# Small products of the identity on TensorE in the idle places of the opening's plan

## The chip, the cores and the metric

The kernel runs on one NeuronCore of a Trainium2 chip. The metric is the time of one execution on the device in microseconds (us). Engines are named as in the profile: PE is TensorE's matmul, PEld its weight load, DVE is VectorE, ACT is ScalarE, POOL is GpSimd, SP is SyncE.

## The reference

The input x has 8 sequences of 256 tokens with 512 features, 2048 tokens in all. Four blocks are added to it one after the other, each on a layer norm of the current x:

```python
x = x + attn_a(layernorm(x))   # here "the stack": 4 layers, 64 wide
x = x + ffn(layernorm(x))      # weights w * (su @ sv), inner 1792, silu(gate) * up, down
x = x + attn_b(layernorm(x))   # 32 query heads, 8 key/value heads of 128, ALiBi, causal
x = x + ffn(layernorm(x))
```

The stack projects 512 features to 64 and then does four times: layer norm, silu, a causal convolution with a complex decaying exponential along the sequence, layer norm, a small feed-forward of 64 to 256 to 64. At the end it norms and projects back to 512 features. All of it is a long chain of small steps.

## The kernel before

The program has three phases. **Phase 1** does the stack, the first feed-forward and what the attention needs ahead; phase 2 is the attention; phase 3 the second feed-forward. No scheduler of a framework orders them. The kernel has a planner of its own, the class `Steps`: a step has a key (name, a, b), an engine, an assumed duration in us, the steps that it comes after, an urgency and the PSUM places that it takes. `Steps.ordered` goes through the steps by assumed time and gives each engine a fixed order, `order1`. It also keeps `ends`, the time at which each step is assumed to end. Each engine then issues its instructions in that order and waits on semaphores before each step. The plan's times decide the order alone; on the chip a step starts when its semaphores allow.

The 2048 tokens are worked on in four blocks of 512. `stack_steps` makes the steps of one block s of the stack. Block 0 is the lead (`lead`), since the first block of the feed-forward can start only when the lead's last layer is done; the blocks 1 to 3 fill in behind. The steps of PE in a layer are, with their lines: `var` (L1900, two products with 128x128 weights and 2 moving columns, for the variance), `rtr` (L1909, four products that spread the reciprocal root), `conv` (L1919 and L1921), `w1` (L1930), `w2` (L1942), and in the lead `idc` (L1914) and `idw` (L1935), which bring the residual in. Between them stand steps of the other engines: `sq` and `silu` and `hid` on ACT, `eps`, `yn`, `ur`, `zr`, `zi`, `pr` on DVE, `rstd`, `ui`, `pi` on POOL. `xT` (L1885) transposes a block's input, `proj` (L1893) projects it, `out` (L1952) projects back. `fxT` (L1810) transposes the normed result for the feed-forward. `scale` (L1794, L1797) makes the low-rank factors of the feed-forward's weights, and `vecc`, `b1f`, `boutf` (L1867, L1872, L1877) fold biases.

The feed-forward's products (`gate`, `up`, `down`) all go through the helper `mm3` (L828), which takes each product as three passes over a high and a low part:

```python
PASSES = ((0, 0), (0, 1), (1, 0))
...
            for stat, mov in pairs:
                for a, b in PASSES:
                    ins = pe.matmul(out_ap, stat[a], mov[b], start=start and n == 0, stop=stop and n == last)
```

Its first two passes thus have the same stationary operand, one right behind the other.

An f32 matmul of the source that is no transpose stands as two MATMUL records in the trace, each with a LDWEIGHTS of its own. `ident` is the 128x128 identity in f32. `DIM` is 64, `PREP` is PSUM bank 5, `SW` is 256. From `("gate", 0, 0)` on, the feed-forward's first product, PE is given the large products of the feed-forward between the small ones of the stack.

Of the kernel before, what the change touches and what calls it, by code (L numbers as in the profile page):

```python
# [22 lines left out]
DEPTH, DIM, DFF = 4, 64, 256  # L23
# [145 lines left out]
def hybrid_block(nc, x_in, win, vecs, b1, w1, w2, wout, bout, ffn_w, lr_long, lr_short, wqkv, wo, qk_w, out, weff_gu, weff_dn, weff_s, weff_q, weff_x):  # L169
    with ExitStack() as ctx:  # L170
# [17 lines left out]
        pe, act, dve, pool, sp = nc.tensor, nc.scalar, nc.vector, nc.gpsimd, nc.sync  # L188
        psum = ctx.enter_context(nc.psum_tensor("psum", [P, 8, 512], F32))
# [3 lines left out]
        ident = place("keep", "ident", [P, P])  # L193
# [86 lines left out]
        SW = BLK // NG2  # L280
        SJ = SW // P
# [346 lines left out]
        follows("dve", ("dlo", end - 1, 0), ("mask", 0, 0), *(("alibi", 0, hd) for hd in range(GRP)))  # L628
        follows("dve", ("dlo", end, 0), ("kw", 0, 0), ("qTlo", 0, 0), ("kTlo", 0, 0), ("qTlo", 0, 1))
        order1["pool"].append(("rel", 0, 0))  # L630

# [119 lines left out]
        def wait_bank(key):  # L753

            for name, a, b in first.before.get(key, ()):
                if name == "fold":
                    pe.wait_ge(fold_dve, FOLD[name, a, b])
                elif name == "aev":
                    pe.wait_ge(a_act, A_ACT[name, a, b])
                elif name == "prcopy":  # L760
                    pe.wait_ge(p1_done, a + 1)
                elif name == "sum":
                    pe.wait_ge(c_done, summed(a, b))
                elif name in ("smul", "fxlo"):
                    pe.wait_ge(aux_free, aux_freed[name, a, b])
                elif name == "hid":
                    pe.wait_ge(stk_act[a], ON_ACT[a][name, b, FC - 1])
                elif name == "xc":
                    pe.wait_ge(stk_act[a], ON_ACT[a][name, b])
                elif name == "xadd":  # L770
                    pe.wait_ge(stk_dve[a], ON_DVE[a][name, b, NG2 - 1])
                else:
                    pe.wait_ge(stk_dve[a], ON_DVE[a][name, b])
# [23 lines left out]
        def row_buffer(key):  # L797
            return F1["xn"][:, first.place[key][1], :]
# [5 lines left out]
        def tile_bank(T, j):  # L804

            return (OWN[0], OWN[1], SUM, SUM + 1)[j] if T == 0 else spare(("fxT", T, j))
# [877 lines left out]
        def dve_phase1():  # L1684
            dve.memset(long_raw, 0.0).then_inc(zero_done, 1)
            step(dve.memset(sm[:], 0.0))
            for what, a, b in order1["dve"]:
# [94 lines left out]
                else:  # L1782
                    dve_ffn(what, a, b)

        def pe_ffn(what, a, b):
            F = F1
            if what == "scale":
# [11 lines left out]
            elif what == "fxT":  # L1799
                if a == 0:  # L1800
                    pe.wait_ge(stk_dve[0], ON_DVE[0]["xadd", SJ - 1, NG2 - 1])
                else:
                    wait_bank((what, a, b))
                bank, xn = tile_bank(a, b), row_buffer(("frow", a, b))
                if a == 0 and b == ON_ACT_ROW:
                    pe.wait_ge(row_act, 1)
                else:
                    pe.wait_ge(row_done, rows_done(a, b))
# [3 lines left out]
            elif what in ("gate", "up"):  # L1812
# [5 lines left out]
                if b == 0 and what == "gate":  # L1818
                    if a == 0:
                        wait_bank((what, a, b))  # L1820
                    if a < IC:
                        pe.wait_ge(gu_lo, g + 1)
                    else:
                        pe.wait_ge(gu_in[r], load_value(a))
                    if a % IC == 0:
                        pe.wait_ge(aux_free, aux_freed["fxlo", T, TPB - 1])
                    if a > 0:
                        pe.wait_ge(gate_done, g)
                elif b == 0 and a > 0:
                    pe.wait_ge(d_done, g)  # L1830
# [27 lines left out]

        def pe_phase1():
            pe.wait_ge(const_done, 10)  # L1860
            for what, a, b in order1["pe"]:
                q, lead = a % SETS, a == 0
                if what in STACK_PE and not lead or what in ("b1f", "boutf"):
                    wait_bank((what, a, b))
                if what == "vecc":
# [1232 lines left out]
```

## Time and profile before

| | |
|---|---|
| median of 3 runs | 2390.9 us (2386.4 to 2393.05) |
| the profiled execution | 2386.13 us |
| its span in the profile | 2384.8 us |
| PE busy | 2340.9 us, 98% |
| PEld busy | 2021.8 us, 85% |
| DVE busy | 1586.9 us, 67% |
| ACT busy | 1209.0 us, 51% |
| POOL busy | 836.9 us, 35% |
| granted TensorE clock, mean over the span | 0.992 |

The 1.33 us between the profiled execution and its span lie outside the span. Busy time is a share of the span, and a mean over phases that differ. A granted clock of 1.00 is 2.4 GHz, one of 0.50 is 1.2 GHz. In the timeline, consecutive instructions of one form are merged into one row with their count; the time in brackets is the idle time of the engine just before the row, and behind the arrow stands what ended it. The busy time of a row of matmuls reaches past the start of the next row, since a matmul's record holds its passage through the array too.

### The profile page before, as it was taken

The numbers are of one execution on the slowest core, as the hardware profiler recorded it, in microseconds if no ns is written. First come the engines' busy times: TensorE is split into PE (matmuls) and PEld (weight loads), VectorE is DVE, ScalarE is ACT, GpSimd is POOL, SyncE is SP. The second block draws the span as 40 slices with busy tenths as digits, with TensorE's granted clock in tenths as the row PEclk, the third lists the DMA queues.
The fourth block names the chain that finished last, engine by engine and source line by source line (L and its number), as shares of the span: only waits on it lengthen the run. The fifth ranks groups of instructions, "written<-read, shape, count | busy, mean of one in ns | idle before, by whom it ended". The sixth has DMA issues, their size and how long they took to land.

```text
span 2384.8 us, 41046 instructions
## 1 busy us (share of the span) xinstructions
PE 2340.9 (98%) x12810; PEld 2021.8 (85%) x12810; DVE 1586.9 (67%) x3892; ACT 1209.0 (51%) x3800; POOL 836.9 (35%) x1332
## 2 busy tenths in 40 slices
PE   6799999999999999999999999999999999999999
PEld 4577777888889999999999999999999978888887
DVE  7666575534267777777777777777777776565553
ACT  6533332233256666666676666666766662132212
POOL 5540343211034355444454554444544440011000
PEclk8999999999999999999999999999999999999999
DMA  4335458987830634535446345454462215565554
GB/s 145 103 137 196 166 214 297 355 334 274 339 145 32 252 122 159 227 149 211 172 153 234 130 159 221 154 208 170 155 234 93 111 62 197 197 221 189 190 194 159
DMA packets 92628, 444.85 MB, mean 187 GB/s; under 512 B 10168, under 2 KB 17336, under 8 KB 72704
## 3 DMA queue, kind: packets, MB, share of 16 engines
q1 hardware_dynamic: 91056, 440.78, 49.8%
q8 instruction: 107, 1.75, 0.3%
q10 hardware_dynamic: 1360, 1.46, 0.2%
q14 instruction: 105, 0.86, 0.1%
HBM read 342.59 MB, written 99.61 MB: 185 GB/s over the span
## 4 chain that ended last, share of the span: by engine, by line
PE 95%; DVE 1%; DMA 1%; ACT 1%; POOL 1%; issue 1%; SPq 0%; DVEq 0%; ACTq 0%; POOLq 0%
PE psum L828 81%; PE psum L2794 4%; PE psum L2756 2%; PE psum L2788 1%; PE psum L1909 1%; PE psum L1930 1%; PE psum L2789 1%; PE psum L2747 1%; PE psum L1942 1%; DMA wD<-weff_dn 1%; PE psum L1900 1%; DMA short_raw<-in_lr_short 0%; PE psum L1794 0%; PE psum L1810 0%; PE psum L1919 0%
## 5 line engine op out<-in xcount | busy, mean ns | idle before, releaser
L828 PE MATMUL psum<-qw,xs 128*128 128x384 f32 x2688 | 548.0, 346 | 0.2 <-DVE su L2600 0.2
L828 PEld LDWEIGHTS psum<-qw,xs 128*128 128x128 f32 x2688 | 457.0, 188 | 1.0 <-issue 0.4
L2573 POOL TENSOR_SCALAR prob<-prob,rsum 128x128 f32<-128x128 f32 (+1 forms) x512 | 230.5, 463 | 528.3 <-DVE rsum L2681 528.1
L2515 ACT ACTIVATE prob<-biased,nmax 128x256 f32<-128x256 f32 (+1 forms) x512 | 227.1, 445 | 151.8 <-DVE nmax L2671 148.6
L2689 DVE TENSOR_TENSOR oT_l<-psum,oT_h 128x512 fp32r<-128x512 f32 x128 | 88.5, 692 | 194.6 <-ACT oT_h L2527 194.6
L828 PE MATMUL psum<-wo_h,oT_h 128*128 128x512 f32 x512 | 208.5, 407 | 1.7 <-issue 1.7
L828 PE MATMUL psum<-wo_l,oT_h 128*128 128x512 f32 x512 | 203.2, 397 | 0.0
L828 PE MATMUL psum<-wo_h,oT_l 128*128 128x512 f32 x512 | 202.3, 395 | 0.0
L2456 ACT ACTIVATE squares<-cc 128x128 f32<-128x128 f32 x512 | 154.3, 305 | 40.6 <-DVE cc L2603 30.5
L2522 ACT ACTIVATE pT_h<-psum 128x384 fp32r<-128x384 f32 x256 | 125.2, 489 | 74.3 <-PE psum L2794 71.8
L2539 POOL TENSOR_TENSOR rr<-ss,mneg_half 128x6 f32<-128x6 f32 (+1 forms) x128 | 150.2, 1173 | 10.7
L828 PE MATMUL psum<-xT0h,wgu 128*128 128x512 f32 x448 | 151.2, 398 | 1.5 <-DVE xT0l L1509 1.5
L828 PE MATMUL psum<-xw_h,wS 128*128 128x512 f32 x448 | 147.0, 389 | 0.0
L828 PE MATMUL psum<-xT1h,wgu 128*128 128x512 f32 x448 | 146.9, 394 | 0.0
L2684 DVE TENSOR_TENSOR pT_l<-psum,pT_h 128x384 fp32r<-128x384 f32 x256 | 141.6, 553 | 7.0 <-ACT pT_h L2522 0.8
L2669 DVE SCALAR_TENSOR_TENSOR low_bias<-alibi,q_root,psum 128x128 f32<-128x128 f32 x256 | 88.5, 346 | 48.7 <-PE psum L2789 47.2
L2794 PE MATMUL psum<-ident,prob 128*128 128x128 f32 x768 | 118.0, 275 | 2.0 <-POOL prob L2573 1.9
L828 PEld LDWEIGHTS psum<-wo_h,oT_l 128*128 128x128 f32 x512 | 96.2, 188 | 23.5
L828 PE MATMUL psum<-xw_h,wA 128*128 128x512 f32 x336 | 112.6, 389 | 0.8 <-issue 0.8
L828 PEld LDWEIGHTS psum<-wo_h,oT_h 128*128 128x128 f32 x512 | 96.4, 188 | 19.3 <-issue 2.3
L828 PE MATMUL psum<-kT,qT_h 128*128 128x256 f32 x512 | 109.3, 295 | 0.0
L828 PEld LDWEIGHTS psum<-wo_l,oT_h 128*128 128x128 f32 x512 | 96.6, 189 | 14.4
(352 smaller groups left out, 5860.6 us busy)
## 6 DMA issues: line engine op xcount, KB each, us to landing
xs<-weff_x SPq DMA_DIRECT2D x62, 1792.0 KB, 7.8
wgu<-weff_gu SPq DMA_DIRECT2D x42, 1024.0 KB, 7.4
qw<-weff_q SPq DMA_DIRECT2D x56, 768.0 KB, 7.9
weff_q<-q_parts SPq DMA_DIRECT2D x84, 384.0 KB, 2.5
wD<-weff_dn SPq DMA_DIRECT2D x56, 512.0 KB, 4.7
wS<-weff_s SPq DMA_DIRECT2D x28, 1024.0 KB, 6.8
wdn<-weff_dn SPq DMA_DIRECT2D x42, 512.0 KB, 4.4
weff_gu<-wgu SPq DMA_DIRECT2D x14, 1024.0 KB, 4.2
```

The lines of the kernel that those rows point to most:

```text
L828: ins = pe.matmul(out_ap, stat[a], mov[b], start=start and n == 0, stop=stop and n == last)
L1900: ins = pe.matmul(psum[:, bank, j * NG2:(j + 1) * NG2], buf_b[q][:, j * P:(j + 1) * P], blk_mean[:], start=True, stop=True)
L2456: ins = act.activation(squares[:, first_place + hd, :], cc[:, tile, half, (hd + 1) * HD:(hd + 2) * HD], ACT.Square, accum_out=ss[:, n:n + 1])
L2515: act.activation(prob[:, b, lo:hi], biased[:, b % 2, lo:hi], ACT.Exp, bias=nmax[:, b, t:t + 1], scale=-1.0, accum_out=esum[:, b, t:t + 1]) ...
L2522: act.activation(pT[0][:, b % 2, :], psum[:, b, 0:SC], ACT.Copy).then_inc(pT_hi, 1)
L2539: pool.tensor_tensor(rr[:, part], ss[:, part], mneg_half[:, 0:part.stop - part.start], ALU.pow).then_inc(r_done if b else r_part, 1)
L2573: pool.tensor_scalar(prob[:, b, lo:hi], prob[:, b, lo:hi], rsum[:, b, t:t + 1], 1.0, ALU.mult, ALU.mult).then_inc(prob_done, 1)
L2669: dve.scalar_tensor_tensor(out=low_bias[:, b % 2, :], in0=alibi[:, b, 0:P], scalar=q_root[:, b:b + 1], in1=psum[:, b, SC:SC + P], op0=ALU. ...
L2684: dve.tensor_tensor(pT[1][:, b % 2, :], psum[:, b, 0:SC], pT[0][:, b % 2, :].bitcast(F32), ALU.subtract).then_inc(pT_lo, 1)
L2689: dve.tensor_tensor(oT[1][:, hs, :], psum[:, 2 * b, :].rearrange("p (h c) -> p h c", h=2), oT[0][:, hs, :].bitcast(F32), ALU.subtract).the ...
L2756: ins = pe.transpose(psum[:, across_bank(what, a, b), hd * P:(hd + 1) * P], q_heads(b)[:, hd // 2, hd % 2, :], ident[:])
L2794: ins = pe.transpose(psum[:, b, k * P:(k + 1) * P], prob[:, b, k * P:(k + 1) * P], ident[:])
```

## The change

After the plan of phase 1 is made, a new function looks through PE's steps in the order of their planned ends. Wherever the plan leaves PE idle for more than 0.3 us after the lead's transposes and before the first `gate` step begins to be due, it enters a number of products for the step that ends the idle time: the planned idle time less 0.1 us, divided by 0.11 us. `keep_busy` issues that many matmuls with `ident` as the stationary operand and 64 columns of `ident` as the moving one. They stand in PE's order directly ahead of the step's own waits and matmuls, and wait for nothing themselves. Their output goes to 64 columns of PSUM that nothing reads before they are written anew: of bank 5 for steps up to the lead's last `out`, of the step's own bank for `fxT` of block 0 and the first `gate`.

```diff
+        def idle_products():
+
+            ends = sorted((first.ends[k], k) for k in order1["pe"] if k in first.ends)
+            found, free = {}, first.ends["xT", 0, 0]
+            for e, k in ends:
+                start = e - first.steps[k][1]
+                if free < first.ends["gate", 0, 0] and start - free > 0.3:
+                    found[k] = int((start - free - 0.1) / 0.11)
+                free = max(free, e)
+            return found
+        IDLE = idle_products()
...
+        def keep_busy(place, key):
+
+            for _ in range(IDLE.get(key, 0)):
+                pe.matmul(place, ident[:], ident[:, 0:DIM], start=True, stop=True)
+
         def pe_ffn(what, a, b):
...
                 bank, xn = tile_bank(a, b), row_buffer(("frow", a, b))
+                if a == 0:
+                    keep_busy(psum[:, bank, 0:DIM], (what, a, b))
...
                         wait_bank((what, a, b))
+                        keep_busy(psum[:, bank, 0:DIM], (what, a, b))
...
-            for what, a, b in order1["pe"]:
+            spare_end = order1["pe"].index(("out", 0, SJ - 1))
+            for n, (what, a, b) in enumerate(order1["pe"]):
                 q, lead = a % SETS, a == 0
+                if n <= spare_end:
+                    keep_busy(psum[:, PREP, SW:SW + DIM], (what, a, b))
```

The order of the steps stays the same on every engine. PE's order has 26 groups of these products more, 179 products in all: in turn 6, 9, 17, 6, 2, 9, 6, 8, 7, 2, 6, 6, 4, 7, 3, 3, 8, 6, 4, 13, 4, 2, 6, 6, 9 and 20. Three places for which the table holds products too (9, 3 and 3) lie behind the lead's last `out`, and none are issued there. The lines of the changed kernel are shifted by up to 24; its product of the identity is L1801.

The first place is PE's order right after the lead's projection, with the variance (L1900, now L1924) and the reciprocal root (L1909, now L1933) of the lead's first norm. Before:

```order
L1893 MATMUL psum<-stack_xT_124,win_c 64x256 x8
L1900 MATMUL psum<-blk_mean,buf_b_84 128x2 x2
L1914 MATMUL psum<-h_76,ident 128x256
L1909 MATMUL psum<-ident,srstd 64x128 x4
L1877 MATMUL psum<-wout_sb,vec 128x512
L1885 MATMUL psum<-ident,xn 128x128 x4
L1919 MATMUL psum<-buf_c_88,center_s 128x256
L1921 MATMUL psum<-buf_b_84,center_s 128x256
```

And with the change:

```order
L1917 MATMUL psum<-stack_xT_124,win_c 64x256 x8
L1801 MATMUL psum<-ident 128x64 x6
L1924 MATMUL psum<-blk_mean,buf_b_84 128x2 x2
L1938 MATMUL psum<-h_76,ident 128x256
L1801 MATMUL psum<-ident 128x64 x9
L1933 MATMUL psum<-ident,srstd 64x128 x4
L1901 MATMUL psum<-wout_sb,vec 128x512
L1801 MATMUL psum<-ident 128x64 x17
L1909 MATMUL psum<-ident,xn 128x128 x4
L1943 MATMUL psum<-buf_c_88,center_s 128x256
L1945 MATMUL psum<-buf_b_84,center_s 128x256
L1801 MATMUL psum<-ident 128x64 x6
L1924 MATMUL psum<-blk_mean,buf_b_84 128x2 x2
```

Four groups have come in between: 6 products ahead of the lead's `var`, 9 ahead of its `rtr`, 17 ahead of the transpose for block 1 and so ahead of the lead's `conv` behind it, and 6 ahead of the next `var`.

The second place is PE's order at the end of the opening, from the lead's `out` (L1952, now L1976) to the first product of the feed-forward (L828, now L841). Before:

```order
L1952 MATMUL psum<-wout_sb,buf_e_96 128x512 x4
L1900 MATMUL psum<-blk_mean,buf_b_85 128x2 x2
L1909 MATMUL psum<-ident,srstd 64x128 x4
L1893 MATMUL psum<-stack_xT_125,win_c 64x256 x8
L1909 MATMUL psum<-ident,srstd 64x128 x4
L1900 MATMUL psum<-blk_mean,buf_b_87 128x2 x2
L1810 MATMUL psum<-ident,xn 128x128 x8
L1909 MATMUL psum<-ident,srstd 64x128 x4
L1810 MATMUL psum<-ident,xn 128x128 x8
L828 MATMUL psum<-xT0h,wgu_103 128x512
```

And with the change:

```order
L1976 MATMUL psum<-wout_sb,buf_e_96 128x512 x4
L1924 MATMUL psum<-blk_mean,buf_b_85 128x2 x2
L1933 MATMUL psum<-ident,srstd 64x128 x4
L1917 MATMUL psum<-stack_xT_125,win_c 64x256 x8
L1933 MATMUL psum<-ident,srstd 64x128 x4
L1924 MATMUL psum<-blk_mean,buf_b_87 128x2 x2
L1801 MATMUL psum<-ident 128x64 x9
L1830 MATMUL psum<-ident,xn 128x128 x8
L1933 MATMUL psum<-ident,srstd 64x128 x4
L1830 MATMUL psum<-ident,xn 128x128 x8
L1801 MATMUL psum<-ident 128x64 x20
L841 MATMUL psum<-xT0h,wgu_103 128x512
```

Here 9 products stand ahead of the first transpose for the feed-forward (L1810, now L1830), and 20 ahead of its first product.

## Rows read from the trace of the kernel before

**Rows 1.** Busy time by stage: range, its length, busy us (instructions) of each engine, PEclk, DMA share, GB/s

```profile
20.00:117.10 97.10, 75.20 (x467) 50.60 (x467) 70.49 (x156) 66.29 (x140) 49.87 (x76) 0.84 0.29 104
...
150.00:2384.00 2234.00, 2224.45 (x12111) 1940.17 (x12109) 1478.25 (x3644) 1123.46 (x3625) 753.43 (x1197) 1.00 0.51 191
```

**Rows 2.** The same view, the four stretches of the opening with the clock halved

```profile
23.30:40.40 17.10, 14.15 (x52) 9.20 (x54) 12.40 (x38) 14.81 (x32) 7.08 (x13) 0.50 0.23 94
...
47.20:50.60 3.40, 3.40 (x20) 1.64 (x15) 2.99 (x6) 2.69 (x6) 1.76 (x3) 0.50 0.00 0
...
74.50:81.40 6.90, 5.65 (x26) 3.69 (x28) 3.17 (x5) 3.56 (x6) 2.79 (x3) 0.51 0.62 227
...
112.10:115.50 3.40, 3.40 (x20) 2.52 (x18) 2.41 (x5) 1.76 (x3) 2.33 (x3) 0.51 0.00 0
```

**Rows 3.** Costliest groups of the page: the joint product's matmuls and their weight loads

```profile
L828 PE MATMUL psum<-qw,xs 128*128 128x384 f32 x2688 | 548.0, 346 | 0.2 <-DVE su L2600 0.2
L828 PEld LDWEIGHTS psum<-qw,xs 128*128 128x128 f32 x2688 | 457.0, 188 | 1.0 <-issue 0.4
```

**Rows 4.** PE's instructions in order of time: start, us, engine, line, operation, [idle before]; clock 1.00

```profile
52.52 0.59 PE L1921 MATMUL psum<-buf_b,center_s 128*128 128x256 f32 x2
52.95 0.59 PE L1900 MATMUL psum<-blk_mean,buf_b 128*128 128x2 f32 x4
53.41 0.47 PE L1797 MATMUL psum<-short_st,long_st 96*128 96x512 f32 x1
```

**Rows 5.** The same view, PE from 23 to 47 us, the rows ahead of which products are put

```profile
23.51 1.01 PE L1900 MATMUL psum<-blk_mean,buf_b 128*128 128x2 f32 x4 [3.55 <-ACT buf_b L1422]
24.38 1.20 PE L1914 MATMUL psum<-h,ident 128*128 128x256 f32 x2
26.04 1.12 PE L1909 MATMUL psum<-ident,srstd 128*64 128x128 f32 x8 [0.46 <-POOL srstd L1253]
...
30.98 1.08 PE L1885 MATMUL psum<-ident,xn 128*128 128x128 f32 x4 [1.81 <-ACT xn L1408]
...
34.24 1.01 PE L1900 MATMUL psum<-blk_mean,buf_b 128*128 128x2 f32 x4 [0.47 <-ACT buf_b L1429]
...
41.77 1.14 PE L1942 MATMUL psum<-hidden,w_c 128*64 128x256 f32 x8 [0.29 <-ACT hidden L1444]
43.60 0.61 PE L1900 MATMUL psum<-blk_mean,buf_b 128*128 128x2 f32 x4 [0.69 <-ACT buf_b L1432]
...
46.68 0.67 PE L1909 MATMUL psum<-ident,srstd 128*64 128x128 f32 x8 [0.96 <-POOL srstd L1253]
```

**Rows 6.** The same view, PE from 63 to 118 us

```profile
63.08 0.61 PE L1900 MATMUL psum<-blk_mean,buf_b 128*128 128x2 f32 x4 [1.14 <-ACT buf_b L1432]
...
64.88 0.63 PE L1885 MATMUL psum<-ident,xn 128*128 128x128 f32 x4 [0.54 <-ACT xn L1408]
...
69.75 0.58 PE L1900 MATMUL psum<-blk_mean,buf_b 128*128 128x2 f32 x4 [0.73 <-ACT buf_b L1422]
70.61 0.67 PE L1919 MATMUL psum<-buf_c,center_s 128*128 128x256 f32 x2 [0.28 <-DVE buf_c L1766]
...
75.13 1.12 PE L1909 MATMUL psum<-ident,srstd 128*64 128x128 f32 x8 [0.85 <-POOL srstd L1253]
76.87 2.08 PE L1930 MATMUL psum<-buf_e,w_sb 64*128 64x256 f32 x8 [0.61 <-DVE buf_e L1743]
...
89.20 0.63 PE L1885 MATMUL psum<-ident,xn 128*128 128x128 f32 x4 [1.29 <-ACT xn L1408]
...
95.64 2.00 PE L1930 MATMUL psum<-buf_e,w_sb 64*128 64x256 f32 x16 [0.61 <-DVE buf_e L1743]
...
103.01 1.99 PE L1952 MATMUL psum<-wout_sb,buf_e 64*128 64x512 f32 x8 [0.61 <-DVE buf_e L1743]
...
111.39 1.33 PE L1810 MATMUL psum<-ident,xn 128*128 128x128 f32 x8 [0.90 <-DVE xn L1497]
...
117.14 0.47 PE L828 MATMUL psum<-xT0h,wgu 128*128 128x512 f32 x1 [1.50 <-DVE xT0l L1509]
```

## The prediction

> **What bounds the kernel now.** I read the stages first. From 150 us to the end PE is busy 2224.45 of 2234 us [rows 1]: there the time is the sum of PE's work, the change leaves that work as it is, and whatever the opening loses or gains moves the end by the same amount. In the opening, from 20 us to the start of the first feed-forward product at 117.14 us, PE is busy only 75.20 of 97.10 us, at a mean clock of 0.84 [rows 1]. DVE (70.49), ACT and POOL are not full either: the stretch is bound by the chain of small steps of the lead, which goes from engine to engine. The reader is to see in the timeline that PE's idle time comes in pieces of 0.3 to 3.6 us, each ended by ACT, DVE or POOL, ahead of a step of the lead more often than not [rows 5, 6]. Such a chain has two handles for this change: a matmul on it is faster at full clock, and it starts later if something stands ahead of it on PE.
>
> **The clock.** Four stretches of the opening ran at 0.50, that is 1.2 GHz instead of 2.4: 23.3 to 40.4, 47.2 to 50.6, 74.5 to 81.4 and 112.1 to 115.5 us [rows 2], 30.8 us in all. The first follows the longest idle piece, 3.55 us before 23.51 [rows 5]; before the fall at 74.5 PE had only short idle pieces, such as 0.73 and 0.28 us at 69.75 and 70.61 [rows 6], so the clock falls in thinly filled stretches too, not only after a long pause. In the four stretches PE was busy 14.15 + 3.40 + 5.65 + 3.40 = 26.6 us [rows 2]. If the products keep the clock at its upper level throughout, that work takes half as long: a gain of at most **13.3 us**. I take all of it, since a lead step or one directly ahead of it on PE makes up nearly all of it, and since the products fill almost every piece.
>
> **What one product costs.** The plan counts 0.11 us. That is the price of its 64 moving columns: L1921, 128x128 weights and 256 columns, takes 0.43 us from its start to the next row's [rows 4], and a quarter of that is 0.107 us. But a product also loads its weights. L1900 has the same weight shape and just 2 moving columns, so it is a weight load and little else. Its two products, four records, take from 52.95 to 53.41 [rows 4]: 0.115 us a record, **0.23 us a product**, at full clock. At half clock the two products at 23.51 take until 24.38 [rows 5], 0.435 us each. That the same identity is loaded again and again spares nothing, as far as the trace tells: the joint products use one stationary operand in two passes running, and there are as many weight loads as matmuls, 2688 and 2688 [rows 3]. So the two bounds of the price are 0.107 (load hidden or left out, streaming alone) and 0.23 us (load visible, streaming hidden under it); I take 0.23, since L1900 is the nearer row in shape. The Trainium skill, TensorE: Matmul & The Clock Gate, section LDWEIGHTS, says that a load takes its columns divided by 1.2 GHz, 107 ns for 128, which as an estimate is 0.21 us for the two loads of a product; the trace agrees with 0.115 us a record.
>
> **The sum.** 179 products by 0.23 are 41.2 us of PE. For each place I take the idle time in brackets at its row, and 0.15 us for the tail of the row before (L1900 at 52.95 is busy 0.59 and the next starts after 0.46; L1921 0.59 against 0.43 [rows 4]). What the products take beyond that delays the step behind them:
> - 18 places have idle time. In order, from 23.51 to 46.68 (products 6, 9, 17, 6, 9, 6, 8 [rows 5]), the excess is 0; 9 x 0.23 - 0.46 - 0.15 = 1.46; 1.95; 0.76; 1.63; 0.54; 0.73: together 7.1 us. From 63.08 to 103.01 (products 6, 4, 7, 3, 8, 6, 13, 6, 6 [rows 6]) it is 0.09, 0.23, 0.73, 0.26, 0.84, 0.62, 1.55, 0.62, 0.62: together 5.6. At the two last places, 111.39 (9 products) 1.02, and 117.14 (20 products, 4.6 us, against 1.50 + 0.15) 2.95: together 4.0.
> - 8 places have no idle time in the trace, though the plan has: 2, 7, 2, 6, 3, 4, 4 and 2 products, 30 in all, 6.9 us in full.
>
> That is 7.1 + 5.6 + 4.0 + 6.9 = **23.6 us** later. 23.6 against a gain of 13.3 leaves **+10.3 us**. Two smaller terms go against each other, and I leave both at nothing: where a product group holds up a step that is not on the lead (the transposes at 30.98, 64.88 and 89.20), later idle time on PE can take up part; and the half clock may return for a stretch, because the first piece of 3.55 us is filled by just 6 products, 1.4 us. Then the 9 and 17 products behind it cost 0.435 us each instead of 0.23 for a while, 26 x 0.2 = 5 us more at most, beside about 2 us of the gain.
>
> On the profiled execution's terms this is 2386.1 + 10.3 = 2396.4 us. The median of the runs shown lies 4.8 us above that execution, and I predict the median: 2390.9 + 10.3 = **2401.2 us**. Nothing else is touched: no wait, no DMA, no order on DVE, ACT, POOL or SP. In the stage after 117 us there are no products. Their output goes to PSUM that nobody waits for, so no engine waits for them; what is queued behind them is PE's next step, and for that DVE's `eps` and `yn`, ACT's `hid` and POOL's `rstd` wait, each of which the lead needs.
>
> A measurement of this kernel can tell about 0.3% from no change, 7.2 us. The forecast is just past that.
>
> **Rivals.**
> - **A product costs only its moving columns, as the plan assumes (faster).** With 0.107 us, 179 are 19.2 us, and the excess over the same idle pieces is 4.6 us, most of it at the 8 places without idle time. Against 13.3 us of clock this is -8.7: 2382.2 us. The two lines cross at about 0.17 us a product, where the excess is 13.4. For it speaks that loads do go on beside matmuls (L1921's 0.43 us shows nothing of its load), and that all these products have one and the same stationary operand; against it L1900 and the 2688 loads [rows 3, 4]. The Trainium skill has a rule that would lead here, in the same page under Back-to-back issue gap: at full clock the gap is the moving columns over 2.4 GHz plus 2.5 ns, 29 ns for 64 columns, or as an estimate 0.06 us for a product of two records. By it nearly all products would vanish in the idle pieces; the row of L1900 does not agree, with 0.115 us a record. Worked out from rows, a product that hides wholly in the pieces leaves 2390.9 - 13.3 = 2377.6 us, too. Chance of this rival: 0.12, of which 0.03 for the products that vanish.
> - **The clock does not follow (much slower).** The products stream only 64 columns per 128 that they load, which no long run of rows in this trace does; if the clock stays down in spite of them, the half-clock stretches stay. Then there is no gain, and the 66 or so products that lie in them (9, 17, 6, 2, 9, 7, 6 and most of 9) cost 0.435: 13 us more. The sum is 23.6 + 13 = +37, 2427 us; if half of it comes true, about +23, 2414 us. For it: the clock stayed at half from 23.3 to 40.4 while PE was busy 83% of the time [rows 2]. Against it: with products in the gaps PE is issuing all the time. Chance: 0.14, mostly for the half.
> - **The excess is taken up (same).** If the lead has slack at more places than I think, for instance because ACT is what it waits for at 30.98 and 89.20 and the products are ahead of transposes, half of the excess is lost in later pieces, and 12 against 13 is nothing: 2390 us. Chance: 0.10.
> - **The products do nothing.** They are in PE's order and nothing removes them, so I give that no chance of its own.
>
> **How the numbers follow.** The forecast has 0.64. Its own range comes from its terms: a gain of 9 to 13.3, an excess of 19 to 26: +6 to +17, likeliest between 2396 and 2408 us. The whole range must leave out no more than 2 in 10: from 2387 us, which takes in the taken-up case and the upper edge of rival A, to 2415, which takes in the half of the clock rival. Slower by over 0.3% (above 2398.1 us): three quarters of the forecast, 0.47, and 0.13 of the clock rival, 0.60. Faster by over 0.3% (below 2383.7): some 0.6 of rival A, 0.07. Within: 0.33.
>
> **What would show it.** In the profile of the changed kernel: the row of the 20 products before the first L841 is about 4.6 us long at full clock (0.23 each; rival A: 2.1 us), with two matmul and two load records for each product. PE is busy nearly all of the time from 20 us to the first L841, which starts near 127 us instead of 117.14 (rival A: 108; clock rival: 140 or more). The granted clock is 1.00 from about 27 us on, and the idle rows at `var`, `rtr` and `w1` are gone; instead DVE's and POOL's idle time before `eps` and `rstd` ends by PE. From there to the end nothing differs. The prediction is wrong if the products' row gives 0.15 us each or less, or if half-clock stretches of more than 10 us remain.

## The result and the profile after

The changed kernel takes 2402.41 us, the median of 10 runs (2393.61 to 2405.71), against 2390.14 us for the kernel before (10 runs, 2386.4 to 2394.18). The ratio, which here and below is estimated from all runs and is not that of the two medians (1.0051), is 1.0044, with a 95% interval of 1.0035 to 1.0054: slower by 0.44%. The forecast was 2401.2 us. Its point and its sign were right. The two terms that it was added up from were both too large, and a third one was left at nothing; the three errors nearly cancel.

The page of the changed kernel begins:

```profile
span 2404.4 us, 41761 instructions
...
PE 2377.8 (99%) x13168; PEld 2065.2 (86%) x13168; DVE 1586.8 (66%) x3892; ACT 1210.0 (50%) x3800; POOL 837.6 (35%) x1332
```

PE is busy 2377.8 us instead of 2340.9. It has 358 records more, two for each of the 179 products. The opening, which answers to the first of [rows 1], and two stretches of its clock, which answer to [rows 2], from the view by stage (columns: range, its length, busy us (instructions) of PE, PEld, DVE, ACT, POOL, PEclk, DMA share, GB/s):

```profile
20.00:136.20 116.20, 111.63 (x821) 93.84 (x820) 72.49 (x160) 66.97 (x141) 51.35 (x78) 0.88 0.24 86
25.30:49.20 23.90, 23.90 (x106) 20.44 (x107) 10.27 (x32) 12.82 (x26) 5.94 (x11) 0.51 0.07 29
49.20:97.00 47.80, 46.82 (x387) 39.19 (x386) 35.76 (x65) 32.48 (x71) 23.12 (x27) 1.00 0.41 139
```

From 20 us to the first feed-forward product PE is now busy 111.63 of 116.20 us, where it was 75.20 of 97.10. Behind that nothing changed: from the first feed-forward product to the end of the span it is 2404.4 - 136.49 = 2267.9 us, and it was 2384.8 - 117.14 = 2267.7. The whole loss is in the opening. The clock is the surprise: from 25.3 to 49.2 us PE was busy all 23.90 us, and the mean granted clock was 0.51 (the stretch at half clock is 25.6 to 49.5 us). There were 17.1 us of half clock in this part before [rows 2], while PE was busy only 83% of the time.

PE in order of time, the rows that answer to [rows 5]:

```profile
19.50 1.55 PE L1801 MATMUL psum<-ident 128*128 128x64 f32 x12
23.44 0.61 PE L1924 MATMUL psum<-blk_mean,buf_b 128*128 128x2 f32 x4 [2.39 <-ACT buf_b L1435]
...
24.50 2.89 PE L1801 MATMUL psum<-ident 128*128 128x64 f32 x18
27.32 1.12 PE L1933 MATMUL psum<-ident,srstd 128*64 128x128 f32 x8
28.37 2.07 PE L1901 MATMUL psum<-wout_sb,vec 64*128 64x512 f32 x2
30.38 7.51 PE L1801 MATMUL psum<-ident 128*128 128x64 f32 x34
37.68 1.06 PE L1909 MATMUL psum<-ident,xn 128*128 128x128 f32 x4
...
52.52 1.08 PE L1966 MATMUL psum<-hidden,w_c 128*64 128x256 f32 x8
```

And those that answer to the end of [rows 6]:

```profile
120.22 1.99 PE L1976 MATMUL psum<-wout_sb,buf_e 64*128 64x512 f32 x8
```

```profile
132.10 4.58 PE L1801 MATMUL psum<-ident 128*128 128x64 f32 x40
136.49 0.48 PE L841 MATMUL psum<-xT0h,wgu 128*128 128x512 f32 x1
```

Of the idle times in [rows 5] one is left, the 2.39 us ahead of L1924. The price of a product stands here: 20 of them from 132.10 to 136.49 are 0.22 us each, at full clock; the 17 from 30.38 to 37.68 are 0.43 us each, at half. The 17 alone fill 7.3 us, where before there were 1.81 us of idle time. By the lead's first `w2` (52.52 instead of 41.77 us) 10.8 of the 19.4 us are lost, and by the last `out` (120.22 instead of 103.01) 17.2.

What PE still waits for between 20 and 136 us, where the columns are the waiting line and its releaser, us in total, times, longest:

```profile
PE psum L1924 <- ACT buf_b L1435: 2.4, 1, 2.4
PE psum L1917 <- DVE svar L1750: 0.7, 1, 0.7
PE psum L1909 <- ACT xn L1421: 0.6, 1, 0.6
PE psum L1924 <- DVE h L1733: 0.5, 1, 0.5
PE psum L1933 <- POOL srstd L1266: 0.3, 1, 0.3
```

That is 4.5 us of idle time, where PE had 97.10 - 75.20 = 21.9 us of it before [rows 1]. The profiled run is the slowest of the ten (2405.71 us), and the profiled execution of before (2386.13 us) lies below all ten of its runs. So their difference, 19.6 us, is more than the 12.3 us between the medians. The ten runs of the changed kernel fall into two groups, three from 2393.6 to 2395.2 us and seven from 2402.2 to 2405.7 us.

### The profile page after: what moved, and what is told of

The parts are those of the page before. It is cut to its first block, busy times and chain, and to the rows that moved or that the text cites. A ratio compares the mean times of both kernels' runs of the same rounds, so it can differ in the third digit from the quotient of the medians.

```text
span 2404.4 us, 41761 instructions
## 1 busy us (share of the span) xinstructions
PE 2377.8 (99%) x13168; PEld 2065.2 (86%) x13168; DVE 1586.8 (66%) x3892; ACT 1210.0 (50%) x3800; POOL 837.6 (35%) x1332
## 4 chain that ended last, share of the span: by engine, by line
PE 97%; DMA 1%; DVE 1%; POOL 0%; issue 0%; ACT 0%; SPq 0%; DVEq 0%; ACTq 0%; POOLq 0%
PE psum L841 81%; PE psum L2818 4%; PE psum L2780 2%; PE psum L1801 2%; PE psum L2812 1%; PE psum L1933 1%; PE psum L1954 1%; PE psum L1966 1%; PE psum L2813 1%; PE psum L1924 1%; PE psum L2771 1%; DMA wD<-weff_dn 0%; PE psum L1812 0%; DMA short_raw<-in_lr_short 0%; PE psum L1943 0%
## 5 line engine op out<-in xcount | busy, mean ns | idle before, releaser
L841 PE MATMUL psum<-qw,xs 128*128 128x384 f32 x2688 | 548.0, 346 | 0.2 <-DVE su L2624 0.2
L841 PEld LDWEIGHTS psum<-qw,xs 128*128 128x128 f32 x2688 | 457.2, 188 | 1.0 <-issue 0.4
L841 PE MATMUL psum<-wo_h,oT_h 128*128 128x512 f32 x512 | 208.6, 407 | 1.8 <-issue 1.7
L841 PE MATMUL psum<-wo_l,oT_h 128*128 128x512 f32 x512 | 203.2, 397 | 0.0
L841 PE MATMUL psum<-wo_h,oT_l 128*128 128x512 f32 x512 | 202.2, 395 | 0.0
L841 PE MATMUL psum<-xT0h,wgu 128*128 128x512 f32 x448 | 151.2, 398 | 0.0
L841 PE MATMUL psum<-xw_h,wS 128*128 128x512 f32 x448 | 147.0, 389 | 0.0
L841 PE MATMUL psum<-xT1h,wgu 128*128 128x512 f32 x448 | 147.0, 394 | 0.0
L2693 DVE SCALAR_TENSOR_TENSOR low_bias<-alibi,q_root,psum 128x128 f32<-128x128 f32 x256 | 88.4, 345 | 48.8 <-PE psum L2813 47.1
L841 PEld LDWEIGHTS psum<-wo_h,oT_l 128*128 128x128 f32 x512 | 96.1, 188 | 23.6
L841 PE MATMUL psum<-xw_h,wA 128*128 128x512 f32 x336 | 112.6, 389 | 0.8 <-issue 0.8
L841 PEld LDWEIGHTS psum<-wo_h,oT_h 128*128 128x128 f32 x512 | 96.4, 188 | 19.3 <-issue 2.3
L841 PE MATMUL psum<-kT,qT_h 128*128 128x256 f32 x512 | 109.3, 295 | 0.0
L841 PEld LDWEIGHTS psum<-wo_l,oT_h 128*128 128x128 f32 x512 | 96.6, 189 | 14.4
```

Source lines behind the costliest of these rows:

```text
L2693: dve.scalar_tensor_tensor(out=low_bias[:, b % 2, :], in0=alibi[:, b, 0:P], scalar=q_root[:, b:b + 1], in1=psum[:, b, SC:SC + P], op0=ALU. ...
```

## The experiments

Each ratio below is against the kernel before on the same chip; the chips differ between experiments, and the median of the kernel before lay between 2388.95 and 2390.14 us on them. In each experiment the place of the output is as wide as the moving columns, and the diffs show the main lines only. The half-clock stretches are those of one profiled run of each kernel. The theory: the loss is the excess of the products over the idle time, at the price of their weight loads, and the clock decides how much of it comes back. The rivals: a product costs its moving columns; the clock depends only on PE being busy; the early or the late products alone make the loss.

**1. What a product costs, and what lifts the clock: 1 moving column.**

```diff
-                pe.matmul(place, ident[:], ident[:, 0:DIM], start=True, stop=True)
+                pe.matmul(place, ident[:], ident[:, 0:1], start=True, stop=True)
```

> Same 179 products, but each with 1 moving column instead of 64. Theory (a product costs its two weight loads, 0.23 us at full clock and 0.43 at half, and the 64 columns stream beneath): each product still costs 0.22 to 0.23 us at full clock, and the time is that of the changed kernel, 2398 to 2410 us, or above if the clock is held down longer. Rival (a product costs its moving columns): the products shrink to less than 0.1 us each, the first feed-forward product starts before 117 us, and the time is below 2390 us.

Measured: 2437.13 us, 1.0203 [1.0185, 1.0221]. PE in order of time:

```profile
31.56 7.41 PE L1801 MATMUL psum<-ident 128*128 128x1 f32 x34
38.83 1.09 PE L1909 MATMUL psum<-ident,xn 128*128 128x128 f32 x4
```

```profile
69.11 1.62 PE L1801 MATMUL psum<-ident 128*128 128x1 f32 x14
70.60 0.68 PE L1943 MATMUL psum<-buf_c,center_s 128*128 128x256 f32 x2
```

A product with 1 column costs the same as one with 64: 34 records in 7.27 us at half clock, 0.43 us a product, and 14 records in 1.49 us at full clock, 0.21 us. So the moving columns are not what a product costs, and that rival is out. For the load, and against a fixed price of a record, speaks L1933 in the changed kernel: its records have 64 weight columns instead of 128, and 8 of them take from 27.32 to 28.37 us, 0.13 us each at half clock, against 0.215 for a record of the products. But the time went up by 48 us instead of 12. Two stretches of the opening show why:

```profile
20.00:100.00 80.00, 79.36 (x455) 65.76 (x455) 44.81 (x103) 46.33 (x98) 29.17 (x55) 0.69 0.27 97
100.00:165.00 65.00, 63.43 (x388) 52.20 (x389) 29.45 (x60) 21.42 (x44) 23.68 (x28) 0.71 0.11 37
```

PE was busy 99% and 98% of the time, with a mean clock of 0.69 and 0.71, and the products took 56 of the 145 us. The theory had the price right and the time only in its clause "or above if the clock is held down longer": with 1 moving column in a product the clock was at half for 87 us of the opening, with PE hardly ever idle.

**2. The same, with 128 moving columns.**

```diff
-                pe.matmul(place, ident[:], ident[:, 0:DIM], start=True, stop=True)
+                pe.matmul(place, ident[:], ident[:], start=True, stop=True)
```

> Same 179 products, but each with 128 moving columns instead of 64. If the load is what a product costs, its 128 columns (0.107 us a record by a quarter or half of the 256-column rows) just fit beneath the load, and a product stays at 0.22 to 0.24 us at full clock. Theory on the clock (it does not rise on rows that are mostly weight load, since in the changed kernel PE was busy without a break from 25.3 to 49.2 us at the half clock): with twice the columns in the same time the clock rises earlier, the first half-clock stretch is under 14 us instead of 23.9, and the time falls by 5 to 8 us to about 2395. Rival (the clock does not depend on what streams, only on PE being busy): the half stretch stays near 24 us and the time at 2398 to 2406 us.

Measured: 2395.06 us, 1.0026 [1.0016, 1.0035], and all ten runs lie between 2394.81 and 2396.06. The lead's projection, the 34 records, the first feed-forward product and the stage:

```profile
19.39 3.68 PE L1917 MATMUL psum<-stack_xT,win_c 128*64 128x256 f32 x16
23.00 2.07 PE L1801 MATMUL psum<-ident 128*128 128x128 f32 x12
...
29.53 4.06 PE L1801 MATMUL psum<-ident 128*128 128x128 f32 x34
33.43 0.60 PE L1909 MATMUL psum<-ident,xn 128*128 128x128 f32 x4
...
42.97 1.08 PE L1966 MATMUL psum<-hidden,w_c 128*64 128x256 f32 x8
...
125.78 0.48 PE L841 MATMUL psum<-xT0h,wgu 128*128 128x512 f32 x1
```

```profile
24.00:125.80 101.80, 99.61 (x824) 83.42 (x822) 70.38 (x148) 62.85 (x135) 48.02 (x58) 1.00 0.24 83
```

A product costs 0.23 us (3.90 us for 17), as with 64 columns or with 1. The clock is at full speed from 24 us on without a break. Three kernels with the same instructions at the same places and the same price of a product at full clock thus give 2437, 2402 and 2395 us, for 1, 64 and 128 moving columns, or ratios of 1.0203, 1.0044 and 1.0026. All that differs is how many columns a product streams and writes, so the rival by which a busy PE is enough is out. It is 1 column against the others that shows it; the intervals of 64 and 128 columns just touch, at 1.0035, and experiments 4 and 8 tell such a pair apart more clearly. The three runs of the changed kernel near 2394 us lie where this one lies. The mean granted clock of every run is on record and fits that: 0.999 in these three, and 0.998 to 0.999 in the ten runs here. Of the seven slower ones five have 0.993 to 0.995, the mark of a long stretch at half clock. The other two have 0.999 as well, which experiment 11 explains.

**3. Fewer products, by the right price.**

```diff
-                    found[k] = int((start - free - 0.1) / 0.11)
+                    found[k] = int((start - free - 0.1) / 0.23)
```

> The planned idle time is divided by 0.23 us instead of 0.11, so that about half as many products (some 80) stand at the same places. Theory: the excess over the idle pieces falls from about 23 us to 6 or 7, most of it at the places that have no idle time on the chip; the clock is at half for 20 to 30 us in the opening, so little of the 13 us comes back: 2390 to 2397 us. Rival (the excess is not what costs; half-clock stretches do): with fewer products the clock is held down more, and the time stays at 2400 us or more.

Measured: 2389.30 us, 1.0002 [0.9993, 1.0010]: no difference from the kernel before. The first feed-forward product starts at 119.75 us. The half-clock stretches are still 22.3 to 42.8 and 49.6 to 56.5 us. No clock has been won, and nearly all of the excess has gone. The theory gave 2390 to 2397 us, and 2389.30 lies just under it; the rival that half-clock stretches alone cost is out, since they are as long as with the changed kernel (27.4 us against 27.3) and the time is some 12 us less.

**4. The same 179 products as one record each,** on a copy of the identity in fp32r, a rounded f32 format. ACT makes the copy at the start, and PE waits for it once.

```diff
+        ident_r = sb1("ident_r", [P, P], F32R)
...
+            act.activation(ident_r[:], ident[:], ACT.Copy).then_inc(ident_r_done, 1)
...
-                pe.matmul(place, ident[:], ident[:, 0:DIM], start=True, stop=True)
+                pe.matmul(place, ident_r[:], ident_r[:, 0:DIM], start=True, stop=True)
```

> Same 179 products, on a copy of the identity rounded to fp32r (one ACT copy at the start, one wait more on PE), so that each is one matmul record with one weight load instead of two. Theory: a product costs 0.115 us at full clock, what the plan assumes; the excess falls from about 23 us to about 5, and what remains is the clock: 2383 to 2392 us. If the clock is held at half as long as in the changed kernel, nearer 2392; if it stays up, nearer 2383. Rival (the number of PE instructions or the writes to PSUM cost, not the loads): above 2398 us.

Measured: 2390.93 us, 1.0008 [0.9999, 1.0017]. The group that took 7.30 us:

```profile
31.57 3.83 PE L1805 MATMUL psum<-ident_r 128*128 128x64 f32 x17
35.22 1.11 PE L1914 MATMUL psum<-ident,xn 128*128 128x128 f32 x4
```

17 records in 3.65 us at half clock are 0.215 us each. The number of products is that of the change and the loss is gone, so it is what a product costs on PE, two records with a load each or one, and not the number of products. In this run the clock was at half up to 38.5 us, and once more from 48.8 to 55.6.

**5 and 6. The early products alone, and the late ones alone.**

```diff
+        at = order1["pe"].index(("w2", 0, 0))
+        IDLE = {k: n for k, n in IDLE.items() if order1["pe"].index(k) <= at}
```

(and `>` in the other.)

> Only the first six groups, 49 of the 179 products, up to the lead's first w2. In the changed kernel the lead's first w2 starts 10.8 us later than before (52.52 against 41.77 us), since these products lie under the half clock and cost 0.43 us each. Theory: that is kept, and behind it the kernel is the one before: +6 to +11, 2396 to 2401 us. Rival (the early delay is taken up by later idle time): 2392 us or less.

> Only the last twenty groups, 130 products. Theory: the opening up to 42 us is as before, with its half-clock stretch of 17 us; behind it the products keep the clock up and take back most of 13.7 us at half clock (at most 6 us of gain), against an excess of about 16 us: +6 to +11, 2396 to 2401 us, so that the early and the late part each make about half of the loss. Rival (the late products pay for themselves): 2392 us or less.

Measured: the early ones 2391.25 us, 1.0010 [0.9997, 1.0023], with a wide spread from 2386.87 to 2400.05; the late ones 2396.85 us, 1.0033 [1.0021, 1.0045]. The theory had both at 6 to 11 us. The late 130 products cost 6.9 us in the median of five runs, which is within it; the early 49 cost 1.3 us in the median, below its range and within noise of nothing, though the profiled run, at 2399.37 us, shows the loss (the same 34 records, 7.3 us):

```profile
34.78 7.51 PE L1803 MATMUL psum<-ident 128*128 128x64 f32 x34
42.09 1.06 PE L1911 MATMUL psum<-ident,xn 128*128 128x128 f32 x4
```

In that run the clock was at half up to about 46 us. That the early products cost as much as the clock makes them cost, and that this differs from run to run, fits the spread but is not shown, since the other eleven runs have no profile. All five runs with the late products lie above the median before, the lowest by 3.0 us. The two parts together, 0.10% and 0.33%, make the 0.44% of the change, within their intervals.

**7. Numbers that fit the measured idle time, 78 products of 128 columns.** The numbers are replaced, and the moving columns are those of experiment 2.

```diff
-        IDLE = idle_products()
+        IDLE = {("var", 0, 0): 16, ("rtr", 0, 0): 2, ("xT", 1, 0): 8, ("var", 0, 1): 2, ("w2", 0, 0): 1, ("var", 0, 2): 3,
+                ("rtr", 0, 2): 4, ("var", 0, 4): 5, ("xT", 2, 3): 3, ("var", 2, 0): 3, ("conv", 0, 2): 1, ("rtr", 0, 5): 4,
+                ("w1", 0, 2): 3, ("xT", 3, 2): 6, ("w1", 0, 3): 3, ("out", 0, 0): 3, ("fxT", 0, 0): 4, ("gate", 0, 0): 7}
```

> Products of 128 moving columns, in numbers that fit the idle time that the chip had before at each place (0.23 us each): 16, 2, 8, 2, 1, 3, 4, 5, 3, 3, 1, 4, 3, 6, 3, 3, 4 and 7, 78 in all, and none where it had no idle time. Theory: no excess, and the clock stays up (nothing falls below full speed from 24 us on), so the 26.6 us of work at half clock give back 8 to 13 us: 2378 to 2385 us, faster than both kernels. Rival (the gain of a full clock is small, since the lead waits for DVE, ACT and POOL): 2385 to 2390 us.

Measured: 2385.07 us, 0.9979 [0.9970, 0.9988]. This one is faster than the kernel before. The first products, the first feed-forward product and the stage up to it:

```profile
19.35 3.84 PE L1803 MATMUL psum<-ident 128*128 128x128 f32 x32
...
111.71 0.47 PE L843 MATMUL psum<-xT0h,wgu 128*128 128x512 f32 x1 [0.19 <-DVE xT0l L1524]
```

```profile
20.00:111.70 91.70, 82.42 (x620) 62.69 (x619) 69.61 (x156) 65.62 (x140) 48.88 (x75) 0.98 0.31 110
```

The first feed-forward product starts at 111.71 us, 5.4 us earlier than before, at a mean clock of 0.98 instead of 0.84. The one half-clock stretch left is 3.4 us long, from 69.8. So a nearly full clock with hardly any excess is worth about 5 us here, by the shift of that product and by the medians (2385.07 against 2390.00), not the 8 to 13 of the theory. The time of 2385.07 us lies just above the theory's range, at the lower end of the rival's, by which the lead's waits for DVE, ACT and POOL keep the gain small. In the profiled run the time behind that product is 2272.1 us, where it was 2267.7 before; most of this arises in the last 460 us, where no products stand, and its cause is open.

**8. One record with 256 moving columns, the 179 products of the change.** As 4, with

```diff
-                pe.matmul(place, ident_r[:], ident_r[:, 0:DIM], start=True, stop=True)
+                pe.matmul(place, ident_r[:], ident_r[:].rearrange("p (o n) -> p o n", o=1).broadcast_to([P, 2, P]), start=True, stop=True)
```

> The 179 products as one fp32r record each, with 256 moving columns instead of 64 (the identity twice, by a step of zero). Theory: 256 columns of fp32r stream in 0.107 us, just beneath the load, so a product still costs 0.11 to 0.13 us at full clock, and the streaming lifts the clock in the first 30 us, where with 64 columns it stayed at half until 37.5 us: 4 to 7 us faster than with 64 columns, 2383 to 2387 us. Rival (the clock does not depend on what streams): as with 64 columns, 2388 to 2393 us.

Measured: 2382.30 us, 0.9974 [0.9964, 0.9983], a little less than the 2383 to 2387 us expected. It is faster than the kernel before by 0.26%, the lowest ratio of all kernels here, though its interval overlaps those of 7 and 9.

```profile
30.09 2.29 PE L1805 MATMUL psum<-ident_r 128*128 128x256 f32 x17
32.29 0.63 PE L1914 MATMUL psum<-ident,xn 128*128 128x128 f32 x4
...
40.46 1.08 PE L1971 MATMUL psum<-hidden,w_c 128*64 128x256 f32 x8
```

```profile
110.67 2.64 PE L1805 MATMUL psum<-ident_r 128*128 128x256 f32 x20
113.14 0.39 PE L843 MATMUL psum<-xT0h,wgu 128*128 128x512 f32 x1
```

20 products from 110.67 to 113.14 are 0.12 us each, about what the plan had assumed. Against experiment 4 only the moving columns differ, and the ratio is lower by 0.0034, 8 us, with intervals well apart. In the profiled run the clock was down from 22.7 to 29.6 us only.

**9. Both together: one record of 256 columns as in 8, numbers that fit (twice those of 7, 156 in all).**

```diff
-        IDLE = idle_products()
+        IDLE = {("var", 0, 0): 32, ("rtr", 0, 0): 4, ("xT", 1, 0): 16, ("var", 0, 1): 4, ("w2", 0, 0): 2, ("var", 0, 2): 6,
...
```

> The numbers of products that fit the measured idle time (as in r7, twice as many, 156, since each is one fp32r record of 256 moving columns at 0.115 to 0.12 us), none at places without idle time. Theory: r7's fit and r8's streaming together; the first feed-forward product starts at 110 to 112 us, against 111.71 with r7 and 113.14 with r8: 2379 to 2383 us. Rival (both have already taken what a full clock can give, since the lead waits for DVE, ACT and POOL): no better than 2382.3 us of r8 within its spread, or worse by a product that comes late.

Measured: 2384.71 us, 0.9980 [0.9971, 0.9989]. It is no better than 8, and its interval overlaps those of 7 and 8. The first feed-forward product starts at 112.42 us. The expectation of 2379 to 2383 us failed, and the rival holds: 7 and 8 had already taken what a full clock gives. What PE still waits for in the opening is other engines; the three longest:

```profile
PE psum L1916 <- ACT xn L1427: 2.1, 2, 1.1
PE psum L1940 <- POOL srstd L1270: 1.6, 4, 0.8
PE psum L1945 <- DVE h L1745: 1.2, 1, 1.2
```

**10. Only the first pause, 16 products of 128 columns.**

```diff
-        IDLE = idle_products()
+        IDLE = {("var", 0, 0): 16}
```

> 16 products of 128 moving columns at one place only, the 3.55 us pause ahead of the lead's first var; nothing else. If it is this pause that takes the clock down at 23.3 us and the sparse work behind it cannot lift it again, holding it over the pause is worth several us: 2384 to 2388 us. Rival (the sparse work behind takes the clock down anyway, one stretch later): half-clock stretches of more than 15 us remain, 2388 to 2391 us.

Measured: 2393.02 us, 1.0016 [1.0006, 1.0025], slightly slower, and above the ranges of both. The half-clock stretches of its profiled run are 31.6 to 41.8, 48.6 to 52.1, 75.9 to 86.2, 89.6 to 93.0 and 116.9 to 127.1 us. The rival has the clock right: with the pause ahead of the first `var` filled, the clock fell all the same at 31.6 us, during the sparsely filled work behind it, and was at half for 37.5 us in all, though in no single stretch of over 15. Why it came out slower rather than equal isn't settled. In the profiled run the clock had come up late (24.7 us), and the lead's projection ran at half, 16 records in 3.61 us:

```profile
20.52 3.68 PE L1917 MATMUL psum<-stack_xT,win_c 128*64 128x256 f32 x16
24.13 4.12 PE L1801 MATMUL psum<-ident 128*128 128x128 f32 x32
28.09 0.51 PE L1924 MATMUL psum<-blk_mean,buf_b 128*128 128x2 f32 x4
```

**11 and 12. The changed kernel, two runs more.**

> The changed kernel itself, one more look. Its ten runs fell in two groups, 3 at 2393.6 to 2395.2 and 7 at 2402.2 to 2405.7 us. Theory: which group a run falls in is decided by the first half-clock stretch, which lasted 23.9 us in the profiled run of 2405.71 us; a run near 2394 us has the clock up by about 30 us and its lead's first w2 near 43 us as in r2, a run near 2403 has it at half until 45 us or more. Rival: runs of both groups have the same clock, and the difference lies behind 136 us.

> As r11, a second look at the changed kernel, for a run of the other group: near 2394 us with the lead's first w2 near 43 us, or near 2403 us with it at 50 us or later.

Measured, single runs: 2404.51 and 2401.56 us. Both are of the slower group (the second just under its seven), and both have the long half clock at the start: the 34 records take 7.3 us in both, and the lead's first `w2` starts at 53.06 and 50.79 us. Of the first:

```profile
15.85 3.57 PE L1896 MATMUL psum<-vec,w_sb 64*128 64x1 f32 x16
19.35 3.68 PE L1917 MATMUL psum<-stack_xT,win_c 128*64 128x256 f32 x16
...
34.32 7.51 PE L1801 MATMUL psum<-ident 128*128 128x64 f32 x34
41.62 1.06 PE L1909 MATMUL psum<-ident,xn 128*128 128x128 f32 x4
...
49.45 1.13 PE L1954 MATMUL psum<-buf_e,w_sb 64*128 64x256 f32 x8
```

Up to 45.6 us everything runs at half speed: even the lead's projection took 3.68 us, where it took 1.95 in the profiled run before. From then on this run was at full clock, without a break up to 136 us, and its first feed-forward product still starts at 135.42 us. Its mean granted clock reads 0.999 all the same, since no half clock stands on record before the first change: so two of the slower runs can have 0.999 too. The second run came up at 43.1 us and reads 0.995. No profiled run is of the faster group. That its clock came up early is thus an inference from the time and the mean clock, not shown.

The kernels side by side:

| kernel | products x us each (full clock) | first feed-forward product, us | half clock in the opening (profiled run), us | ratio |
|---|---|---|---|---|
| before | 0 | 117.14 | 23.3-40.4, 47.2-50.6, 74.5-81.4, 112.1-115.5 | 1 |
| changed | 179 x 0.22 | 136.49 | 25.6-49.5, 97.3-100.7 | 1.0044 |
| 1: 1 column | 179 x 0.21 | 165.04 | to 23.9, and 87 us in seven stretches from 27.3 on | 1.0203 |
| 2: 128 columns | 179 x 0.23 | 125.78 | to 24.0 | 1.0026 |
| 3: right price | 80 x 0.22 | 119.75 | 22.3-42.8, 49.6-56.5 | 1.0002 |
| 4: one record | 179 x 0.12 | 119.32 | to 38.5, 48.8-55.6 | 1.0008 |
| 5: early only | 49 x 0.22 | 129.79 | to 46, 56.0-62.8, 76.5-83.3, 90.1-93.5, 124.3-127.7 | 1.0010 |
| 6: late only | 130 x 0.22 | 127.91 | 22.6-39.7, 46.5-53.3 | 1.0033 |
| 7: fitted | 78 x 0.23 | 111.71 | 69.8-73.2 | 0.9979 |
| 8: one record, 256 | 179 x 0.12 | 113.14 | 22.7-29.6 | 0.9974 |
| 9: 7 and 8 | 156 x 0.12 | 112.42 | 70.4-73.8 | 0.9980 |
| 10: first pause | 16 x 0.23 | 121.07 | to 24.7, 31.6-41.8, 48.6-52.1, 75.9-86.2, 89.6-93.0, 116.9-127.1 | 1.0016 |

## Why the prediction was right, and where its steps were not

- **What bounds the kernel.** Right. The time behind the first feed-forward product is 2267.9 us in the changed kernel and 2267.7 before, and the loss is the shift of that product.
- **The price of a product, 0.23 us.** Right: 0.22 us at full clock and 0.43 at half. Experiment 1 shows that the moving columns do not count: 1 column costs as much as 64. Experiments 4 and 8 show that a product with one load costs half. One reading on the way was wrong: 0.107 us is not the price of 64 moving columns. In experiment 10 the projection passes 16 records of 256 columns in 3.61 us at half clock, 0.23 us each, so 64 columns take at most 0.06 us of a record there.
- **The excess, +23.6 us.** The term that was too large. Experiments 2 and 7 have the same kind of product, 179 of them and the 78 that fit, both nearly at full clock. Against the kernel before their medians are +6.1 and -4.9 us, so the excess is about 11.0 us. The profiles agree, if the time is taken from the end of the lead's projection, which ran at half clock in experiment 2 and not in 7: from 23.00 to 125.78 it is 102.8 us, from 19.35 to 111.71 it is 92.4, and the excess 10.4. The step that failed took each place for itself, with the idle time of a trace that had long stretches at half clock. At full clock PE's other work is shorter, which leaves more room, and a delay ahead of a step off the lead can be taken up later. How much each of the two gives is not measured.
- **The gain of the clock, 13.3 us.** Too large as well, for two reasons. It needed the clock up all the time, and the clock stayed down for long: the profiled run had 27.3 us of half clock, against 30.8. And a nearly full clock is worth 4.9 us by the medians, 5.4 by the shift of the first feed-forward product (experiment 7): work at double speed does not bring the end forward where it is not on the lead, or where the lead waits for ACT, DVE or POOL. How the 26.6 us of PE's work in those stretches divide, the runs do not show.
- **What was left at nothing.** "The half clock may return for a stretch, because the first piece of 3.55 us is filled by just 6 products" was put at 5 us more at most, beside 2 us of the gain, and not counted. Between the changed kernel and experiment 2, whose clock was up from 24 us on, lie 6.2 us in the medians, near those 7 (4.3 by the ratios, 1.0044 and 1.0026). In the profiled run it was the largest single effect. From the end of the projection the lead's first `w2` comes 33.0 us later there, and 20.0 in experiment 2; the first feed-forward product comes 117.0 us later, and 102.8 in experiment 2: 14.2 us. The mechanism stood in the rival by which the clock does not follow, with products that stream little, but I had it with 0.14 and the price of all stretches. It holds for the first stretch; behind it the clock stayed up but for 3.4 us.
- **The sum.** By the medians it is 11.0 of excess, -4.9 of clock and 6.2 of half clock under the products, +12.3. By the profiled runs it is 10.4 - 4.9 + 14.2 = 19.7 us, from the end of the lead's projection on. That end is 19.50 us in the changed kernel; before it is put at 19.88, since the same 16 records, busy 1.95 us in both, took 1.88 us to the next row in the changed kernel:

```profile
18.00 1.95 PE L1893 MATMUL psum<-stack_xT,win_c 128*64 128x256 f32 x16
```

  The forecast had +23.6 and -13.3. That +10.3 lies near +12.3 is luck in good part: the excess was 12.6 us too large, the gain 8.4 too large, and 6.2 were left out.
- **The signs that were named.** The 20 products take 4.4 us where 4.6 were forecast, with two records each; the first L841 starts at 136.49, not near 127; the clock is not at full from 27 us on. By the text's own test, half-clock stretches of more than 10 us, the account of the clock was wrong, though the time and the sign came out.
- **The rivals.** "A product costs only its moving columns" fell with experiment 1. What it predicts for so low a price, faster than before by 8.7 us, is near what experiment 8 gives, whose products do cost 0.12 us and come with an early full clock: 2382.30 us against 2390.00 before, 7.7 us. "The excess is taken up" was nearer than its 0.10: it had 12 us left of the excess, and 11 were. The Trainium skill, TensorE: Matmul & The Clock Gate, section LDWEIGHTS, puts a load at its columns divided by 1.2 GHz, as an estimate 0.21 us for the two of a product. At full clock the traces agree, with 0.21 to 0.23; at half clock they do not, with 0.43.

## What to carry to other kernels

Work that is put into an engine's idle time has to be priced by what it costs on the chip, its weight load included, and counted by the idle time that a trace shows, not a plan: with 128 columns each, 179 products cost 0.26%, and the 78 that fit gained 0.21%. Filler that is to hold TensorE's clock has to be tried on the chip, for PE being busy was not enough here. At the same 0.21 to 0.23 us a product, 1 moving column left the clock at half for 87 us of the opening, with 64 it came up for good only at 43 to 50 us in three profiled runs (but for one stretch of 3.4 us in one of them), and with 128 it was up from 24 us on. And a clock held up on a chain that other engines bound gave back less than half of what the half clock costs PE: about 5 of 13.3 us.

## What the runs showed of the hardware

PE can be busy without a pause and stay at the half clock: 23.9 us at 0.51 in the changed kernel, and 98 to 99% busy at a mean of 0.70 over 145 us in experiment 1. About half of the first stretch, and 56 us of the second, went to products that load 128 columns of weights twice and stream 64 columns or 1. With more moving columns in the same products the clock was up earlier: from 24.0 us on with 128 (experiment 2), and with records of 256 from 29.6 instead of 38.5 us (experiments 8 and 4). An f32 product that reloads the stationary operand already in place pays for both of its loads in full, 0.22 us at full clock and 0.43 at half. And the column PEclk can read 1.00 where the instructions run at half: before the first change of the clock on record (45.6 us in experiment 11) the rows tell, here the projection with 3.68 us instead of 1.95. Who reads the clock of an opening has to check it against the time of a known row.
